# Routing groups taken one to three steps earlier in a fused attention and expert-routing kernel

## The reference, cut to what matters

```
x = x + tanh(g_xattn) * attention(src=ctx, tgt=layernorm(x))    # 16 heads of 8, 64 keys a sequence
y = layernorm(x)
gates = sigmoid(y @ Wg)                      # 8 experts
top 2 gates of each token, normalised to sum 1 -> w
shared = (silu(y @ Ws1) * (y @ Ws3)) @ Ws2
routed = sum over the two chosen experts e of w_e * (silu(y @ We1[e]) * (y @ We3[e])) @ We2[e]
x = x + tanh(g_ffn) * (shared + routed) / 3
```

## Time and profile before

| | us |
|---|---|
| median of three runs | 461.3 (459.54, 461.4, 461.3) |
| profiled execution | 458.93 |
| its span in the trace | 457.1 |
| PE busy | 359.4 (79%) |
| DVE busy | 344.0 (75%) |
| POOL busy | 279.4 (61%) |
| ACT busy | 264.9 (58%) |

### The profile page before, as it was taken

The page is one execution under the profiler, slowest core; times in us unless marked ns, Lnnn a source line. Parts: engine busy times, 40 slices in busy tenths (PEclk is TensorE's granted clock), DMA queues, the critical chain, the costliest instruction groups (busy, mean ns, idle before and its releaser), DMA issues.

```text
span 457.1 us, 10667 instructions
## 1 busy us (share of the span) xinstructions
PE 359.4 (79%) x3718; PEld 269.3 (59%) x3718; DVE 344.0 (75%) x866; ACT 264.9 (58%) x601; POOL 279.4 (61%) x375
## 2 busy tenths in 40 slices
PE   0689999997998969899869710999999999999400
PEld 0356666665765647676658600777777777778300
DVE  2559999999999998998848820576777777777447
ACT  1257777776687746687656600355555555556244
POOL 3373666666379966888647773017777777777700
PEclk9999999999799988899979865799999999999855
DMA  4920699991001110000001155113236666541179
GB/s 110 275 77 3 261 375 377 391 385 41 13 27 49 36 48 25 27 25 26 25 23 42 49 217 165 52 52 94 93 95 231 232 231 230 210 184 52 47 264 298
DMA packets 39331, 62.36 MB, mean 136 GB/s; under 512 B 5936, under 2 KB 23344, under 8 KB 39280
## 3 DMA queue, kind: packets, MB, share of 16 engines
q1 hardware_dynamic: 32704, 51.12, 32.6%
q0 software_dynamic: 4992, 10.30, 6.7%
q10 hardware_dynamic: 1584, 0.27, 0.4%
HBM read 18.32 MB, written 31.56 MB: 109 GB/s over the span
## 4 chain that ended last, share of the span: by engine, by line
PE 41%; DVE 25%; issue 13%; POOL 13%; ACT 4%; DMA 3%; POOLq 0%; DVEq 0%; SPq 0%; ACTq 0%
POOL expert_rows L545 7%; PE ps L1215 6%; PE ps L1216 5%; PE ps L1217 5%; DVE row_max L935 5%; PE ps L1252 3%; DVE inv_sum L976 3%; PE ps L1158 3%; POOL token_sums L622 3%; PE ps L1112 3%; DVE norm L900 2%; PE ps L1240 2%; PE ps L1238 2%; PE ps L1239 2%; DVE x_sb L1061 2%
## 5 line engine op out<-in xcount | busy, mean ns | idle before, releaser
L622 POOL DMA_INDIRECT token_sums<-prob,y_at x92 | 94.5, 1027 | 60.7 <-DVE prob L1035 38.8
L545 POOL DMA_INDIRECT expert_rows<-c_sb,pos x64 | 64.3, 1005 | 16.9 <-issue 16.8
L587 POOL TENSOR_TENSOR k_mask<-k_st,head_mask 128x512 f32<-128x512 f32 x32 | 33.5, 1046 | 43.8 <-ACT k_st L695 43.6
L739 ACT ACTIVATE h_hi<-prob 128x512 fp32r<-128x512 f32 x62 | 38.3, 634 | 36.5 <-DVE prob L998 36.5
L732 ACT ACTIVATE probT<-ps 128x512 f32<-128x512 f32 x62 | 36.9, 598 | 30.6 <-PE ps L1217 27.0
L1112 PE MATMUL ps<-k_mask,qT 32*64 32x256 f32 x512 | 46.0, 431 | 9.4 <-DVE prob L941 7.7
L998 DVE TENSOR_TENSOR prob<-ps,probT 128x512 f32<-128x512 f32 x62 | 40.2, 684 | 13.9 <-ACT probT L732 10.9
L935 DVE TENSOR_REDUCE row_max<-ps 128x16 f32<-128x1024 f32 x32 | 38.9, 1216 | 11.0 <-PE ps L1112 10.9
L1003 DVE TENSOR_TENSOR h_lo<-prob,h_hi 128x512 fp32r<-128x512 f32 x62 | 40.5, 689 | 3.4 <-ACT h_hi L739 0.4
L1019 DVE TENSOR_TENSOR xT_lo<-ps,xT_hi 128x512 fp32r<-128x512 f32 x23 | 15.9, 692 | 35.9 <-ACT xT_hi L744 35.9
L703 ACT ACTIVATE probT<-ps 128x512 f32<-128x512 f32 x64 | 35.2, 595 | 10.5 <-PE ps L1158 10.4
(11 more groups left out here) (164 smaller groups left out, 977.1 us busy)
## 6 DMA issues: line engine op xcount, KB each, us to landing
expert_rows<-zeros SPq DMA_DIRECT2D x36, 520.0 KB, 5.2
c_sb<-expert_rows SPq DMA_DIRECT2D x23, 260.0 KB, 2.7
wbuf_hi<-w_hi SPq DMA_DIRECT2D x15, 384.0 KB, 2.9
wbuf_lo<-w_lo SPq DMA_DIRECT2D x15, 384.0 KB, 3.4
w_raw<-in_L_ffn_We_dram SPq DMA_DIRECT2D x24, 128.0 KB, 4.2
c_sb<-token_sums SPq DMA_DIRECT2D x8, 256.0 KB, 4.7
xT_lo<-token_sums SPq DMA_DIRECT2D x8, 256.0 KB, 4.9
out_dram<-x_sb SPq DMA_DIRECT2D x8, 256.0 KB, 4.9
```

Of the source, the lines that this page charges most:

```text
L545: pool.indirect_dma_start(out=xs, out_offset=bass.IndirectOffsetOnAxis(pos[:, k, i:i + 1], 0), in_=c_sb[:, i, :], in_offset=None).then_inc ...
L622: pool.indirect_dma_start(out=ys, out_offset=bass.IndirectOffsetOnAxis(y_at[:, s, k:k + 1], 0), in_=yrows[:, s % 2, k * D:(k + 1) * D], in ...
```

## The change

Every group's exponential comes one step earlier (14, 22, 30, 34 become 13, 21, 29, 33); DVE's five parts are done together in steps 14, 22, 30, 34, where A was in 15, 23, 31, 35 and B in 16, 24, 32, 36; counts and places come two steps earlier (17, 25, 33, 37 become 15, 23, 31, 35). Scattering starts in step 15 in place of 18, with one tile a step to step 32 (two in step 32), and only tiles 28 to 31 are left for the units. PE waits for `gate_exp` behind the logits of step 33 and, new, for `pos_ready` ahead of step 35's transpose. The table work is dealt over steps 0 to 3. The last group stays where it is.

```diff
-        GATE_STEP = [14, 22, 30, 34, None]
-        COUNT_STEP = [16, 24, 32, 36, None]
-        RANK_STEP = [17, 25, 33, 37, None]
+        GATE_STEP = [13, 21, 29, 33, None]
+        COUNT_STEP = [14, 22, 30, 34, None]
+        RANK_STEP = [15, 23, 31, 35, None]
@@ scatter_tiles(t)
-            if 18 <= t < NT:
-                return range(t - 18, t - 17)
-            return {NT: [14], NT + 1: [15], NT + 2: [16, 17], NT + 3: [18, 19], NT + 4: [20, 21],
-                    NT + 5: [22, 23]}.get(t, [])
+            if 15 <= t < NT:
+                return range(t - 15, t - 14)
+            return {NT: [17, 18], NT + 1: [19, 20], NT + 2: [21, 22], NT + 3: [23, 24], NT + 4: [25, 26],
+                    NT + 5: [27]}.get(t, [])
@@ POOL step
-                if t == 0:
-                    tables()
+                if 0 <= t < 4:
+                    tables(t)      # part 0: zeros and the first iota; 1: most memsets, iotas; 2: selects; 3: three iotas
@@ POOL unit
-                if n == TAIL_UNIT:
-                    for i in range(24, 28):
-                        scatter(i)
@@ DVE step
-                    if last is not None and last - 1 <= t <= last:
-                        for part in (range(0, 3) if t < last else range(3, 5)):
+                    if t == last:
+                        for part in range(5):
                             routing(g, part)
@@ PE step
+                    pe.matmul(p_logit[:, i, :], xT_f32[:, b, :], wg_raw[:, :], start=True,
+                              stop=True).then_inc(logits_ready, 1)
                     if t > NT and t in GATE_STEP:
                         pe.wait_ge(gate_exp, GATE_STEP.index(t) + 1)
-                    pe.matmul(p_logit[:, i, :], xT_f32[:, b, :], wg_raw[:, :], start=True,
-                              stop=True).then_inc(logits_ready, 1)
@@ PE step, ahead of the transpose of tile t-5
+                    if t > NT + 1 and t in RANK_STEP:
+                        pe.wait_ge(pos_ready, RANK_STEP.index(t) + 1)
```

More of the change, by code:

```diff
@@ L507, in _ @@
             pool.wait_ge(scale_step, 1)
[L509 to L533, removed]
-                exact = dict(channel_multiplier=0, allow_small_or_imprecise_dtypes=True)
-                pool.iota(steps512[:, :, :], [[T, E], [ROWS, JMAX - 1]], base=ROWS, **exact)
-                pool.iota(slot_id[:, :], [[1, DYN]], base=0, **exact)
-                pool.iota(slot_less[:, :], [[1, DYN]], base=1 - JMAX, **exact).then_inc(tables_ready, 1)
@@ new lines, in tables @@
+            def tables(part):
+                exact = dict(channel_multiplier=0, allow_small_or_imprecise_dtypes=True)
+                if part == 0:
+                    pool.memset(zeros[:, :], 0.0).then_inc(zeros_set, 1)
+                    pool.wait_ge(zeros_set, 1)
+                    pool.memset(zeros[:, :].rearrange("p (r d) -> p r d", d=XW)[:, :, D:D + 1], NOWHERE).then_inc(zeros_set, 1)
+                    pool.iota(c_sb[:, :, D].rearrange("p (c k) -> p c k", k=CH), [[CT, NC], [1, CH]], base=0,
+                              channel_multiplier=CH, allow_small_or_imprecise_dtypes=True).then_inc(table_step, 1)
+                if part == 1:
+                    pool.wait_ge(table_step, 1)
+                    pool.tensor_scalar(c_sb[:, :, D], c_sb[:, :, D], 1.0 / T, None, ALU.mult)
+                    pool.iota(nowhere[:, :, :], [[ROWS, SLOTS], [1, CH]], base=2 * T, channel_multiplier=CH,
+                              allow_small_or_imprecise_dtypes=True)
+                    pool.memset(ones[:, :], 1.0)
+                    pool.memset(not_before[:, :], -1.0)
+                    pool.memset(earlier[:, :, :], 1.0)
+                    for b in begins.values():
+                        pool.memset(b[:, :], 1.0)
+                    pool.iota(carry[:, 0, :], [[T // P, E]], base=0, channel_multiplier=0,
+                              allow_small_or_imprecise_dtypes=True).then_inc(table_step, 1)
+                if part == 2:
+                    pool.wait_ge(table_step, 2)
+                    pool.affine_select(out=not_before[:, :], in_=not_before[:, :], compare_op=ALU.is_ge, fill=0.0, base=0,
+                                       pattern=[[-1, P]], channel_multiplier=1)
+                    pool.affine_select(out=earlier[:, :, :], in_=earlier[:, :, :], compare_op=ALU.is_ge, fill=0.0, base=-1,
+                                       pattern=[[1, E], [-1, E]], channel_multiplier=0)
+                    for n, t in begins.items():
+                        pool.memset(t[:, :].rearrange("p (e t) -> p e t", e=E)[:, :, 0:1], 0.0)
+                if part == 3:
+                    pool.iota(steps512[:, :, :], [[T, E], [ROWS, JMAX - 1]], base=ROWS, **exact)
+                    pool.iota(slot_id[:, :], [[1, DYN]], base=0, **exact)
+                    pool.iota(slot_less[:, :], [[1, DYN]], base=1 - JMAX, **exact).then_inc(tables_ready, 1)
```

## The result

The changed kernel takes 470.5 us (median of four) against 460.42 for the kernel before: 1.0214 times as long, 95% interval 1.017 to 1.0258. One of its four executions, of 1108.02 us, was disturbed and is left out of the ratio; the median of the other three is 470.06. I had forecast 460.8 with a range to 464.8. It is 10 us, or 2.1%, slower, and outside the range.

The account below looks back on a forecast made before the run. POOL's backlog of scatters was taken to set the end. Terms -6.4 - 0.5 + 1.9 + 0.1 + 1.9 + 2.45 = -0.55 turned 458.93 into 458.4, plus 2.4 for the median: 460.8 us; range 458.8 to 462.8, with parts of both rivals 456.8 to 464.8.

Parts of the forecast that it names:

- Tail: From last places to first routed rows: only tiles 28-31 left to scatter, last transfer 7.3 us sooner, less 0.9 for weight copies: -6.4.
- Steps 33 to 36: PE waits 2.5 us for the exponential and 4.1 for group 3's places, so the last places come 2.45 us later.
- Start: Dealing out the tables starts tile 2's `k_mask` earlier; part is lost while PE is slow: -0.5 us (0 to -0.9).
- Merged A and B: Group 0's routing on DVE: same instruction time, but B loses its cover (+1.74) and the places' move frees 0.90: net +0.84 us.
- I read 12.55 as PE's: The two steps after group 0's A took 12.55 us, taken as set by PE, with B covered there.
- Net +0.1: Group 1: B uncovered +1.74 us, its places' step falling back -1.6; range -1.4 to +1.7.
- the places' long step: Group 1's step with its places took 7.76 us and was to fall back to 6.18: -1.6.
- Group 2: A and B in the open in steps 30 and 31: +1.74 us, places +0.65, less half a microsecond idle: +1.9 (+0.9 to +2.9).
- Scatters in steps 15 to 17: DVE's work stretches beside POOL in two of these steps, at 0.55 us each: +1.1, counted within group 0's +1.9.
- The slower rival: PE's clock decides: lost in step 33 too (+1.6), group 1 +1.6, group 2's late scores +1.0: 465.0 us, chance 0.25.

## Why the prediction was wrong, point by point

- **Tail, -6.4: right.** Measured -6.55, with POOL idle for 5.99 ahead of the last places, 5.7 forecast. Putting the scatters back lost it again (21.5 us from the last `pos` to the first routed transpose).
- **Steps 33 to 36, +2.45: right in kind, 1 short.** The waits came as worked out (2.41 and 4.11 for 2.5 and 4.1), and up(3) ran at the low clock. Part of up(1) did too (matmuls of 0.63 from 242.09 to 245, behind the wait of 2.41), which I had put in the range and not in the sum. With group 3 back in its old place the kernel is 3.8 faster.
- **Start, -0.5: too small.** -1.7 in the profile, 4.1 timed for the tables alone. I let the low clock eat the gain; in the executions seen, the clock was at 1.00 there, and the one that lost it was one with the tables' wait.
- **"Merged A and B": this step failed.** I priced groups 0, 1 and 2 at 1.9, 0.1 and 1.9; the stages gave 5.5 (with steps 18 to 21), 3.4 and 6.2. Three assumptions fell. (1) "I read 12.55 as PE's", so the two steps behind a merged burst would take 12.55 again. The gap grew from 2.5 in group 0 (I had used group 1's 4.3 for it) and 4.3 in group 1 to 4.66 and 6.47, and the steps took 13.5 and 13.9; with the clock held they take 11.4, shown in group 0 of the kernel with idle work in the gap. So the clock costs 2.1 in group 0, and 12.55, measured at a clock that had fallen to 0.50, was no floor. (2) "Net +0.1" for group 1 refunded the places' long step and left the port to the range; the step with the burst ran 13.89 where the one free of `k_mask` ran 10.61. (3) Group 2: the row maximum of step 31 came 3.1 later behind step 29's than before, for +1.9, and I did not look past it: from it to the first expert product another 3.1 was lost (5.74 for 2.63), as PE worked through step 31 at a granted clock of 0.55. In step 32 a merged burst cost nothing in this stretch; in step 30 it did.
- **Scatters in steps 15 to 17, +1.1: too small.** 3.8 by the kernel with the old scatter steps, of which 1.5 by step 18. The sum also had a slip: 6.18 less 5.53 is 0.65 a step and not 0.55, so it should have read +1.3.
- **The slower rival had the mechanism** (a clock lost behind merged bursts) at 465.0, with 0.25, itself just outside the stated range. What it lacked is that the clock falls after all three bursts, and that the early scatters and the port add to it. Merged bursts in their early steps are what made the kernel slow, since splitting them, with B and the places a step later, takes back 11.5; merging alone in the old steps cost 2.3. How the 11.5 divides is shown for group 0's clock (2.1) and, by a burst free of `k_mask` against two that are not, for POOL beside DVE in group 1 (up to 3.3). The rest is a reading of the traces: the clock falls in the split kernel and in the kernel before too, for less time.
- The Trainium skill's rule on the port (SBUF — State Buffer, "SBUF: two separate sides"), that GpSimd and some VectorE instructions lock one port pair and the loser blocks, deserved a place in the sum: 2.05 for 0.23 beside one `k_mask` agrees with it in kind. The row of the VectorE instruction begins 0.66 us ahead of `k_mask`'s, so which of the two came first is not shown. Its drain on each table switch (ScalarE: Activation LUTs, "What ACT_TABLE_LOAD costs") is again not seen: in the changed kernel PE waited 2.41, not 3.9.

## What to carry to other kernels

Where an in-order engine feeds a pipeline, the same work in one piece can cost more than in two: price the gap that it opens on the others, the clock that they are granted behind it, and what of a third engine lands inside. Put such work under a wait that is there anyway. And before moving work ahead to shorten a queue, look at what the queue's own engine waits for: putting POOL's scatters ahead of one other instruction gave 4.2 us, where moving the routing groups ahead cost 10.

## What the runs showed that I had not expected

- Useless matmuls ahead of a gap or in it made a kernel 11.3 and 5.5 us faster (459.23 and 464.99 for 470.5). The low clock was granted for about 10 and 14 us there, from step 13 to the first expert product, where it was 34.
- With the same kind of filling the clock is kept in one burst and lost in another: 1.00 and 0.73 behind bursts of 11.06 and 13.36 us in the same execution. Ten runs of two of these kernels spread over 454.22 to 459.44 and 460.69 to 466.45 us; whether that is the clock is not shown, as thirteen runs of the kernel before spread over 459.2 to 464.1.
- A tile's two scatters a step cost more right behind a burst than later: steps 16 and 17 took 13.65 with them and 10.92 without, against 6.18 for 5.53 a step in the earlier trace rows. The steps just ahead gave 1.2 of that back.
